# Graph network layers 1 and 2: row exponentials written to DRAM once and loaded spread over all partitions, in place of a spread by TensorE before every quarter

## The chip, the cores and the metric

The kernel runs on one core of one Trainium2 chip. The metric is the device time of one execution in microseconds (us), the median of several runs. TensorE is called PE below, VectorE DVE, ScalarE ACT, GpSimd POOL and SyncE SP. SP does no arithmetic in this kernel; it only issues DMAs.

## The reference

Four graph layers stand one after the other on a node matrix `x` of 4096 x 128 with a 4096 x 4096 adjacency matrix `adj`. Each is fed with `relu(layernorm(x))` and adds its result to `x`.

```python
def _L1_gnn_ref(x, adj, ff0_w, ff1_w, attn_w, g1, b1, g2, b2):   # _ln: normalise, times g, plus b
    x_norm = _ln(x, g1, b1)
    mask = (adj > 0) | jnp.eye(n, dtype=bool)
    for i in range(K):                                             # K = 2 heads
        h = x_norm @ ff0_w[i].T
        s_src = h @ attn_w[i, :c]
        s_dst = h @ attn_w[i, c:]
        e = jax.nn.leaky_relu(s_src[:, None] + s_dst[None, :])
        e = jnp.where(mask, e, jnp.float32(NEG))
        atten = jax.nn.softmax(e, axis=1)
        att = _ln(atten @ h + x, g2, b2)
        h_next = h_next + jax.nn.elu(att @ ff1_w[i].T) / K
    return h_next
...
    Wh = inputs @ W                                                # layer 2 (_L2_gnn_ref)
    e = jax.nn.leaky_relu((Wh @ a[:D])[:, None] + (Wh @ a[D:])[None, :], LRELU_ALPHA)
    att = jax.nn.softmax(jnp.where(adj > 0, e, NEG), axis=-1)
    return jax.nn.relu(att @ Wh)
...
h = jnp.maximum(_layernorm(x, axis=-1), 0.0)
x = x + _L0_gnn_ref(L0_gnn_t, h, adj, ...)       # (degree-normalised adj) @ h, times W, relu
h = jnp.maximum(_layernorm(x, axis=-1), 0.0)
x = x + _L1_gnn_ref(h, adj, ...)
h = jnp.maximum(_layernorm(x, axis=-1), 0.0)
x = x + _L2_gnn_ref(h, adj, ...)
h = jnp.maximum(_layernorm(x, axis=-1), 0.0)
x = x + _L3_gnn_ref(h, adj)                      # adj.T @ h, divided by the column sums
```

## The kernel before

The program names its work by five stages, `run(0, ...)` to `run(4, ...)`: stage 0 is layer 0, stages 1 and 2 are the two heads of layer 1, stage 3 is layer 2 and stage 4 is layer 3. Below, "stage" is always this number. A stage has four quarters `q` of 1024 target nodes each, and a quarter has 32 steps `k`, one for each block of 128 source nodes. All data is float32, apart from the adjacency pattern, which stays in SBUF as the uint8 tile `mask`.

In stages 1 to 3, one step is this. DVE makes a 128 x 1024 tile of unnormalised attention weights, `E = max(R, rank[:, k]) * mask` (L1124), in one of three buffers (`EB = 3`), all part of the tile `ring`. PE multiplies it with the features in `G` and sums in PSUM `acc`: in stages 1 and 2 with the features stationary (L382, two products of 512 columns, each recorded as two instructions), in stages 0, 3 and 4 with the tile stationary (L366, eight products of 129 columns, each recorded as two). `rank` holds an exponential for each source node. `R`, also in `ring`, holds the exponential for each of the quarter's 1024 target nodes, the same row on all 128 partitions: it is what this change is about.

How `R` comes about before the change: for each quarter, ACT copies the quarter's eight columns of `row[h]` to `rq` (`rows_columns`, L772). PE spreads each column over all partitions with a transpose of the column broadcast to 128 x 128 (`spread_rows`, eight transposes, L393) into the PSUM tile `turn`. ACT copies `turn` to `R` in two pieces (`rows_out`, L775 and L776), but not before DVE has made the last tile of the quarter that runs, since that still reads the old `R` (`rows_copy`). There are 14 such spreads: one for each of the 12 quarters of stages 1 to 3 and two more, since the first quarter of stages 1 and 3 has an early row (for its steps 0 to 23, when the last quarter of features is not known) and a late one (steps 24 to 31).

The order on PE is written out by hand. `run(h, q, hooks)` issues the 32 steps, and behind step `k` the hook of that number; the lists `ks` say behind which steps the work of the neighbouring parts stands: `feed` (features of the next stage: `turned` L397 or L409, `project` L420), `post1` (the end of the quarter before: `sums_back` L435, `turned` L397, `apply` L448), and the spreads. DVE has hooks of the same kind. Quarters with a register as index run in a hardware loop (`quarters`). Each engine works in its own order and waits for the others through semaphores: `e_made` (tiles that DVE has made), `e_used` (tiles that PE has read), `rows_spread`, `rows_kept` and so on.

In stages 1 and 3 the first quarter also brings the maximum over all source nodes: DVE's `top_of` (`first`, a maximum over each partition, `second`, the maximum over all, at L1048 after PE's `spread_top`, one transpose).

Of the kernel before, what the change touches and what calls it, by code (L numbers as in the profile page):

```python
# [30 lines left out]
P = 128  # L31
# [33 lines left out]
def graph_layers(nc, x, adj, adj_t, diag, alpha, w0_t, bias0, ff0, ff0_t, ff1_t, attn, g1, b1, g2, b2,  # L65
# [20 lines left out]
    with ExitStack() as ctx:  # L86
# [13 lines left out]
        ident = sb("ident", [P, P])  # L100
        ff1T = sb("ff1T", [P, HEADS, D])
# [19 lines left out]
        w0T = spare[:, 0:D]  # L121
        bias0_b = spare[:, D:2 * D]
# [8 lines left out]
        mean2 = spare[:, o + D + 2:o + 2 * D + 2]  # L131
        fold, later = [spare[:, o + 3 * D + i * S:o + 3 * D + (i + 1) * S] for i in range(2)]
# [34 lines left out]
        kept_rows = {1: 2, 2: 6, 3: 11}  # L167
# [30 lines left out]

        rq_ready, rows_spread, rows_kept = sem("rq_ready"), sem("rows_spread"), sem("rows_kept")
# [70 lines left out]
        def _(sp):  # L270
# [44 lines left out]

            sp.wait_ge(saved, 16 * Q)

            def bring_back(q):
                if fixed(q):
# [37 lines left out]
        def _(pe):  # L357
# [195 lines left out]
            def stage1(q):  # L553
                m = q + kept_rows[1]
# [13 lines left out]
            def stage2(q):  # L568
                m = q + kept_rows[2]
                if fixed(q) and q == 0:  # L570
                    ks = [1, 15, 17, 29]  
                    run(2, q, at(ks, post1(0, Q - 1, m, 2 * Q) + (lambda: spread_rows(m),)))
                    return
# [13 lines left out]
            def spread_mean():  # L587
# [5 lines left out]
            ks = [0, 8, 9, 18, 19, 20, 21, 26, 27]    # L593
            run(3, 0, at(ks, steps + (lambda: spread_top(late_top[3]), lambda: spread_rows(kept_rows[3] - 1), spread_mean,
                                      lambda: spread_rows(kept_rows[3]))))

            def stage3(q):
                run(3, q, {28: lambda: spread_rows(q + kept_rows[3])})
# [831 lines left out]
```

## Time and profile before

| | us |
|---|---|
| median of 3 runs | 1242.03 |
| lowest and highest | 1241.24, 1245.62 |
| the profiled execution | 1240.94 |
| its span | 1239.1 |
| PE busy | 1223.0 (99% of the span) |
| DVE busy | 752.7 (61%) |
| ACT busy | 317.8 (26%) |

Times within the profile count from the start of the span. Stage 1 takes about 262 to 502 us, stage 2 to 759, stage 3 to 1005 and stage 4 to the end. The record of one PE instruction is longer than its share of the engine, since PE begins the next before the last has ended; the distance from one start to the next tells its cost. The chain of work is a view that follows the end of the kernel back to its start, and it gives such distances.

### The profile page before, as it was taken

What the parts mean: (1) busy time and instruction counts of PE and PEld (TensorE: products, weight loads), DVE (VectorE), ACT (ScalarE), POOL (GpSimd) and SP (SyncE); (2) the same over time, 40 slices, a digit from 0 to 9 for tenths busy, and PEclk for the clock granted to TensorE, in tenths of its full rate; (3) what the DMA queues carried; (4) which work ended last, traced back from release to release, by engine and by line L of the source; (5) the groups of instructions that cost most, each with busy time, mean ns of one, the idle gap of its engine ahead of it and who ended that gap; (6) DMA issues with size and microseconds to landing.
All of it is one profiled execution on the core that took longest, in us unless ns stands there. A gap on an engine that the chain in (4) does not pass through costs nothing.

```text
span 1239.1 us, 20060 instructions
## 1 busy us (share of the span) xinstructions
PE 1223.0 (99%) x7953; PEld 967.4 (78%) x7953; DVE 752.7 (61%) x1359; ACT 317.8 (26%) x769; POOL 9.6 (1%) x21
## 2 busy tenths in 40 slices
PE   8999999999999999999999999899999999999998
PEld 8999999964444444444454547899999999999998
DVE  5446554588877777778878787778787840000001
ACT  3312121234433324231424144442312130000000
POOL 3000000000000000000000000000000000000000
PEclk9999999999999999999999999999999999999999
DMA  9888886820000000000000000000000069999810
GB/s 315 275 268 285 281 278 215 275 73 1 17 1 17 0 18 0 17 17 1 1 17 0 17 0 18 1 1 1 1 0 1 1 242 409 410 410 398 294 62 18
DMA packets 47241, 144.33 MB, mean 116 GB/s; under 512 B 4784, under 2 KB 13248, under 8 KB 47168
## 3 DMA queue, kind: packets, MB, share of 16 engines
q1 hardware_dynamic: 42976, 139.08, 31.3%
q10 hardware_dynamic: 3696, 3.67, 0.8%
q8 instruction: 52, 0.85, 0.3%
q0 software_dynamic: 496, 0.55, 0.2%
q14 instruction: 21, 0.17, 0.0%
HBM read 139.09 MB, written 4.19 MB: 116 GB/s over the span
## 4 chain that ended last, share of the span: by engine, by line
PE 87%; DVE 7%; DMA 2%; issue 1%; ACT 1%; SPq 1%; DVEq 0%; ACTq 0%
PE acc L366 51%; PE acc L382 30%; DVE ring L1124 4%; PE mix L420 2%; PE mix L448 1%; PE mix L435 1%; PE turn L397 1%; PE turn L393 1%; ACT V L623 1%; DMA mask<-in_adj_t 1%; SPq L272 1%; DMA mask<-in_adj 1%; DVE stats L960 1%; DVE stats L956 0%; DVE X L1273 0%
## 5 line engine op out<-in xcount | busy, mean ns | idle before, releaser
L1124 DVE SCALAR_TENSOR_TENSOR ring<-ring,score,mask 128x1024 f32<-128x1024 f32 x384 | 482.9, 1281 | 113.1 <-PE acc L382 69.5
L382 PE MATMUL acc<-ring,G 128*128 128x512 f32 x1024 | 450.5, 594 | 3.2 <-DVE ring L1124 2.7
L366 PE MATMUL acc<-G,mask 128*128 128x129 f32 x3584 | 403.5, 275 | 1.6 <-DMA mask<-in_adj 1.1
L366 PEld LDWEIGHTS acc<-G,mask 128*128 128x128 f32 x3584 | 401.5, 192 | 2.1 <-DMA mask<-in_adj 1.5
L382 PEld LDWEIGHTS acc<-ring,G 128*128 128x128 f32 x1024 | 189.3, 190 | 234.0 <-issue 201.5
L366 PE MATMUL acc<-G,ring 128*128 128x129 f32 x2560 | 289.8, 275 | 0.3 <-DVE ring L1124 0.3
L366 PEld LDWEIGHTS acc<-G,ring 128*128 128x128 f32 x2560 | 287.8, 192 | 1.5 <-DVE ring L1124 1.2
L1158 DVE TENSOR_SCALAR mask<-mask 128x1024 uint8<-128x1024 f32 x96 | 64.5, 689 | 53.7 <-DMA mask<-in_adj_t 53.5
L1375 DVE TENSOR_SCALAR zero<-U 128x8 f32<-128x8 f32 x3 | 0.5, 171 | 155.0 <-ACT U L816 155.0
L816 ACT COPY U<-acc 128x387 f32<-128x387 f32 (+1 forms) x36 | 15.6, 446 | 270.9 <-PE acc L366 269.9
L635 ACT ACTIVATE dev<-var 128x8 f32<-128x8 f32 x28 | 5.9, 210 | 266.6 <-DVE var L969 266.6
L1158 DVE TENSOR_SCALAR mask<-ring 128x1024 uint8<-128x1024 f32 x32 | 22.0, 692 | 32.1 <-DMA ring<-in_adj_t 22.2
L623 ACT ACTIVATE V<-X,shift,scale 128x128 f32<-128x128 f32 (+1 forms) x92 | 36.7, 481 | 0.0
L775 ACT COPY ring<-turn 128x512 f32<-128x512 f32 x14 | 8.2, 585 | 109.2 <-DVE ring L1124 64.3
L619 ACT ACT_TABLE_LOAD x26 | 33.4, 1283 | 1.2 <-PEq L1409 0.8
L615 ACT COPY cols<-ident 128x1 f32<-128x1 f32 x40 | 7.6, 190 | 95.8 <-DVE shift L979 35.6
L1394 DVE SCALAR_TENSOR_TENSOR zero<-U 128x3 f32<-128x3 f32 (+1 forms) x3 | 0.5, 161 | 50.8 <-ACT U L816 50.8
L623 ACT ACTIVATE V<-U,shift,scale 128x128 f32<-128x128 f32 x64 | 25.5, 481 | 10.3 <-DVE shift L979 10.3
L420 PEld LDWEIGHTS mix<-ring,U 128*128 128x128 f32 x176 | 20.8, 192 | 2.0 <-issue 1.2
L397 PEld LDWEIGHTS turn<-ident,V 128*128 128x128 f32 x120 | 13.7, 141 | 10.0 <-ACT V L623 5.8
L420 PE MATMUL mix<-ring,U 128*128 128x4 f32 (+2 forms) x176 | 21.0, 265 | 0.0
L397 PE MATMUL turn<-ident,V 128*128 128x128 f32 x120 | 15.7, 274 | 4.1 <-ACT V L623 4.1
(168 smaller groups left out, 548.2 us busy)
## 6 DMA issues: line engine op xcount, KB each, us to landing
mask<-in_adj SPq DMA_DIRECT2D x128, 512.0 KB, 14.9
mask<-in_adj_t SPq DMA_DIRECT2D x96, 512.0 KB, 4.7
ring<-in_adj_t SPq DMA_DIRECT2D x32, 512.0 KB, 4.7
inputs<-V ACTq DMA_DIRECT2D x4, 512.0 KB, 2.7
V<-inputs SPq DMA_DIRECT2D x4, 512.0 KB, 3.9
X<-in_x SPq DMA_DIRECT2D x3, 512.0 KB, 10.6
out_x<-V ACTq DMA_DIRECT2D x3, 512.0 KB, 15.1
X<-in_x SPq DMA_DIRECT2D x2, 256.0 KB, 3.2
```

The lines of the kernel that those rows point to most:

```text
L272: sp.dma_start(X[:, t:t + n, :], x[t * P:(t + n) * P, :].rearrange("(s p) d -> p s d", p=P)).then_inc(loaded, 16)
L366: mm = pe.matmul(acc[:, b, (s % 3) * DW:(s % 3) * DW + DW], lhs[:, s * P:(s + 1) * P], g, start=(k == 0 and s % 3 == 0), stop=(k == T - 1) ...
L382: mm = pe.matmul(acc[:, c, :], g, moving[:, c * BANK:(c + 1) * BANK], start=(k == 0), stop=(k == T - 1), skip_group_check=True)
L393: return pe.transpose(dst, col.broadcast_to([P, P]), ident[:, :])
L397: mm = pe.transpose(turn[:, s * P:(s + 1) * P], V[:, s, :], ident[:, :])
L420: mm = pe.matmul(dst, U[:, s * P:(s + 1) * P], weights, start=True, stop=True, skip_group_check=True)
L435: mm = pe.matmul(mix[:, s // 3, (s % 3) * DW:(s % 3) * DW + DW], U[:, s * P:(s + 1) * P], back_w[h], start=True, stop=True, skip_group_che ...
L619: act.activation(warm[func], ident[:, 0:1], func)
L623: ins = act.activation(dst(s), src(s), func, bias=add(s), scale=mul(s))
L816: act.copy(U[:, b * 3 * DW:b * 3 * DW + w], acc[:, b, 0:w]).then_inc(acc_taken, 1)
L1124: dve.scalar_tensor_tensor(E[k % EB], R, rank[h][:, k:k + 1], span(mask, (q * T + k) * QC, QC), ALU.max, ALU.mult).then_inc(e_made, 1)
L1158: dve.tensor_scalar(span(mask, (q * T + k) * QC, QC), tile0(q, k), 0.0, None, ALU.is_gt).then_inc(mask_made, 1)
```

## The change

Ten of the 14 spreads are gone, those of whole quarters. In their place, three times (once for each of stages 1, 2 and 3), PE turns `row[h]`, 128 x 32, to 32 x 128 in one transpose (`turn_rows`) into `mix`. ACT (stages 1 and 3) or DVE (stage 2) copies that to `turned_rows`; SP writes it to DRAM as 4096 numbers in a row (`write_rows`, 16 KB) and loads from there, for each quarter, the 1024 numbers to all 128 partitions (`load_rows`, 512 KB). They land in `R` or in 1024 columns of `G` that hold nothing at the time (`rows_home`), so that most loads stand a quarter ahead of their use. The early and the late rows of the first quarters of stages 1 and 3 are still spread by PE; the late ones go to a part of `G` (`late_home`), which leaves `R` free for the second quarter's load.

What goes with it: the exponentials `v` of stage 2 move from a column of `G` to `v_second`; a few hooks move by a step or two; DVE's quarters and SP's `bring_back` are no longer in loops; the memset of the last column of `G` for stage 4 is cut in two.

```diff
-        kept_rows = {1: 2, 2: 6, 3: 11}
+        kept_rows = {1: 2, 3: 4}
+        in_third, in_fourth, of_first = [G[:, i, t:t + S, :].rearrange("p s d -> p (s d)")[:, 0:QC]
+                                         for i, t in ((0, 2 * S), (0, 3 * S), (1, 3 * S))]
+        rows_home = {(1, 0): R, (1, 1): R, (1, 2): in_third, (1, 3): in_fourth, (2, 0): R, (2, 1): of_first, (2, 2): R,
+                     (2, 3): of_first, (3, 0): R, (3, 1): R, (3, 2): in_fourth, (3, 3): R}
+        late_home = in_fourth
...
+            def write_rows(h):
+                sp.wait_ge(rows_ready, h)
+                sp.dma_start(given_rows[h - 1].rearrange("(t p) -> t p", p=P), turned_rows).then_inc(rows_written, 16)
+                sp.wait_ge(rows_written, 16 * h)
+
+            def load_rows(h, q):
+                sp.dma_start(rows_home[h, q], given_rows[h - 1, q * QC:(q + 1) * QC].partition_broadcast(P))\
+                    .then_inc(rows_loaded[h, q], 16)
+
+            sp.wait_ge(own_made, Q)
+            write_rows(1)
+            sp.wait_ge(e_made, EARLY)
+            load_rows(1, 1)
+            load_rows(1, 2)
+            sp.wait_ge(e_made, T)
+            load_rows(1, 3)
+            write_rows(2)
+            sp.wait_ge(e_made, 2 * T)
+            load_rows(2, 0)
...
+            sp.wait_ge(*all_summed(1, Q - 1))
+            load_rows(2, 1)
             bring_back(0)
-            quarters(sp, 1, Q - 1, bring_back)
+            sp.wait_ge(e_made, (Q + 1) * T)
+            load_rows(2, 2)
+            bring_back(1)
+            sp.wait_ge(e_made, (Q + 2) * T)
+            load_rows(2, 3)
+            bring_back(2)
+            bring_back(3)
+
+            write_rows(3)
+            sp.wait_ge(e_made, 2 * Q * T + EARLY)
+            load_rows(3, 1)
+            sp.wait_ge(e_made, (2 * Q + 1) * T)
+            load_rows(3, 2)
+            sp.wait_ge(e_made, (2 * Q + 2) * T)
+            load_rows(3, 3)
...
+            def turn_rows(h):
+                pe.wait_ge(r_made, h)
+                pe.transpose(mix[0:T, 2, 0:P], row[h], ident[:, :]).then_inc(rows_turned, 1)
...
-                    ks = [17, 18, 19, 21, 22, 25, 26]  
+                    ks = [17, 18, 19, 21, 22, 24, 26]
                     run(1, q, at(ks, own + (lambda: spread_top(late_top[1]), lambda: spread_rows(1), spread_fold,
-                                            lambda: spread_top(late_top[2]), lambda: spread_rows(m))))
+                                            lambda: turn_rows(1), lambda: (pe.wait_ge(rows_ready, 1), spread_top(late_top[2])))))
                 else:
-                    ks = [2, 15, 17, 29]  
-                    run(1, q, at(ks, post1(0, q - 1, m, 2 * Q) + (lambda: spread_rows(m),)))
+                    ks = [2, 15, 17]
+                    run(1, q, at(ks, post1(0, q - 1, m, 2 * Q)) | more)
             stage1(0)
-            stage1(1)
+            stage1(1, {24: lambda: turn_rows(2)})
+            pe.wait_ge(rows_ready, 2)
...
-                    ks = [1, 13, 15, 26, 29, 27]  
-                    run(2, q, at(ks, steps + (lambda: spread_rows(m, q + 2 * Q),)))
+                    ks = [1, 13, 15, 26, 28]
+                    run(2, q, at(ks, steps))
...
-            ks = [0, 8, 9, 18, 19, 20, 21, 26, 27]  
+            ks = [0, 8, 9, 18, 19, 20, 21, 26, 24]
             run(3, 0, at(ks, steps + (lambda: spread_top(late_top[3]), lambda: spread_rows(kept_rows[3] - 1), spread_mean,
-                                      lambda: spread_rows(kept_rows[3]))))
+                                      lambda: turn_rows(3))))
...
+            def keep_turned(h):
+                act.wait_ge(rows_turned, h)
+                act.copy(turned_rows, mix[0:T, 2, 0:P]).then_inc(rows_ready, 1)
...
             late_rows(1)
-            next_columns(1, 1)
-            feed(2, 2 * Q, 0, [lambda: put_right(1), lambda: exponentials(2), lambda: rows_copy(1, 1)])
+            keep_turned(1)
+            feed(2, 2 * Q, 0, [lambda: put_right(1), lambda: exponentials(2)])
...
-                dve.wait_ge(rows_kept, q + kept_rows[h] - (1 if early else 0))
+                if early:
+                    dve.wait_ge(rows_kept, kept_rows[h] - 1)
+                else:
+                    dve.wait_ge(rows_loaded[h, q], 16)
...
-            quarters(dve, 1, Q - 2, stage3, st, STAGE3)
-            stage3(Q - 1)
+            for q in range(1, Q):
+                stage3(q)
+            dve.wait_ge(e_made, 3 * Q * T)
+            st.mark(dve.memset(G[:, 0, EARLY:T, D], 1.0))
```

Three places in the order of instructions follow. The changed file has other line numbers: its L432 is L382 of before, L443 is L393, L470 is L420, L447 is L397. The first is PE in the first quarter of stage 1, from the spread for the late sums (`fold`) to the end of the quarter; two rows of `acc<-ring,G` are one step, `cols` is `spread_top`, `rq` the row for the second quarter. Before:

```order
L393 MATMUL mix<-ident,ring 128x128 x8
L382 MATMUL acc<-ring,G 128x512 x6
L393 MATMUL mix<-ident,cols 128x128
L382 MATMUL acc<-ring,G 128x512 x2
L393 MATMUL turn<-ident,rq 128x128 x8
L382 MATMUL acc<-ring,G 128x512 x16
```

The same place in the changed kernel:

```order
L443 MATMUL mix<-ident,ring 128x128 x8
L432 MATMUL acc<-ring,G 128x512 x4
L605 MATMUL mix<-ident,score 32x128
L432 MATMUL acc<-ring,G 128x512 x4
L443 MATMUL mix<-ident,cols 128x128
L432 MATMUL acc<-ring,G 128x512 x16
```

The eight transposes of `rq` are gone, one transpose of the whole `row[1]` stands behind step 24, and the transpose of `cols`, for which DVE waits, stands behind step 26 and not 25.

The second place is ACT at the same point of the program, from the copy of the late row. Before:

```order
L775 COPY ring<-turn 128x512
L776 COPY ring<-turn 128x512
L746 COPY U<-mix 128x512
L747 COPY U<-mix 128x512
L772 COPY rq<-score 128x8
L615 COPY cols<-ident 128x1
L623 ACTIVATE V<-X,norms 128x128 x8
L671 DMA inputs<-V 128x1024
L760 ACTIVATE score<-score,cols 128x24
L764 ACTIVATE G<-G,cols 128x1032 x3
```

And in the changed kernel:

```order
L829 COPY G<-turn 128x512
L830 COPY G<-turn 128x512
L800 COPY U<-mix 128x512
L801 COPY U<-mix 128x512
L834 COPY ring<-mix 32x128
L670 COPY cols<-ident 128x1
L678 ACTIVATE V<-X,norms 128x128 x8
L726 DMA inputs<-V 128x1024
L814 ACTIVATE score<-score,cols 128x24
L818 ACTIVATE G<-G,cols 128x1032 x3
```

The copy of the turned rows (L834), which waits for PE's step 24 and the transpose behind it, stands where ACT copied eight columns without a wait, and the normalisation, the save to DRAM and the scaling of `G` (`put_right`) are queued behind it.

The third place is PE at the end of a looped quarter of stage 2, from the turn of the next stage's input. Before:

```order
L397 MATMUL turn<-ident,V 128x128 x8
L483 REGISTER_ALU
L382 MATMUL acc<-ring,G 128x512 x2
L266 REGISTER_ALU
L393 MATMUL turn<-ident,rq 128x128 x8
L483 REGISTER_ALU
L382 MATMUL acc<-ring,G 128x512 x2
L483 REGISTER_ALU
L382 MATMUL acc<-ring,G 128x512 x2
L420 MATMUL mix<-ring,U 128x130 x8
```

And in the changed kernel:

```order
L447 MATMUL turn<-ident,V 128x128 x8
L533 REGISTER_ALU
L432 MATMUL acc<-ring,G 128x512 x2
L533 REGISTER_ALU
L432 MATMUL acc<-ring,G 128x512 x2
L465 REGISTER_ALU
L470 MATMUL mix<-ring,U 128x130 x8
L533 REGISTER_ALU
```

The spread is gone, and the projection into `mix` stands one step earlier, two steps behind the turn.

## Rows read from the trace of the kernel before

**Rows 1.** The page: busy time, share of the span, instructions; granted clock in 40 slices.

```profile
PE 1223.0 (99%) x7953; PEld 967.4 (78%) x7953; DVE 752.7 (61%) x1359; ACT 317.8 (26%) x769; POOL 9.6 (1%) x21
PEclk9999999999999999999999999999999999999999
```

**Rows 2.** The page: chain that ended last, shares of the span by engine.

```profile
PE 87%; DVE 7%; DMA 2%; issue 1%; ACT 1%; SPq 1%; DVEq 0%; ACTq 0%
```

**Rows 3.** Group of spreading transposes on PE: busy us, mean ns, idle before.

```profile
L393 PE MATMUL turn<-ident,rq 128*128 128x128 f32 x112 | 14.6, 273 | 0.5 <-ACT rq L772 0.5
```

**Rows 4.** Chain through a quarter of stage 1: start us, us, what.

```profile
440.95 0.87 PE turn L393 x8
441.82 8.72 PE acc L382 x20
...
501.34 0.88 PE turn L393 x8
```

**Rows 5.** Chain in stages 0 and 3.

```profile
123.39 51.92 PE acc L366 x464
...
941.49 0.87 PE turn L393 x8
942.36 57.19 PE acc L366 x512
```

**Rows 6.** Order of time, PE, end of stage 1's first quarter: start us, us.

```profile
309.49 3.69 PE L382 MATMUL acc<-ring,G 128*128 128x512 f32 x8 [0.27 <-DVE acc L1073]
313.02 0.27 PE L393 MATMUL mix<-ident,cols 128*128 128x128 f32 x1
313.13 1.88 PE L382 MATMUL acc<-ring,G 128*128 128x512 f32 x4
```

**Rows 7.** The same for DVE; in brackets the idle time before and its releaser.

```profile
313.57 0.28 DVE L1048 TENSOR_REDUCE cols<-mix 128x1 f32<-128x128 f32 x1
...
314.17 2.47 DVE L1124 SCALAR_TENSOR_TENSOR ring<-ring,score,mask 128x1024 f32<-128x1024 f32 x2
317.64 1.28 DVE L1124 SCALAR_TENSOR_TENSOR ring<-ring,score,mask 128x1024 f32<-128x1024 f32 x1 [1.00 <-PE acc L382]
...
322.89 1.28 DVE L1124 SCALAR_TENSOR_TENSOR ring<-ring,score,mask 128x1024 f32<-128x1024 f32 x1 [0.63 <-PE acc L382]
```

**Rows 8.** The same for ACT.

```profile
308.02 0.59 ACT L747 COPY U<-mix 128x512 f32<-128x512 f32 x1
...
312.61 3.23 ACT L764 ACTIVATE G<-G,cols 128x1032 f32<-128x1032 f32 x3
...
320.73 0.58 ACT L775 COPY ring<-turn 128x512 f32<-128x512 f32 x1 [4.26 <-DVE ring L1124]
```

**Rows 9.** Chain at the end of a quarter of stage 2.

```profile
620.65 0.87 PE turn L393 x8
...
628.24 1.28 ACT L772
...
630.27 3.70 PE acc L382 x8
```

**Rows 10.** Order of time, DVE, the same place.

```profile
628.61 1.28 DVE L1124 SCALAR_TENSOR_TENSOR ring<-ring,score,mask 128x1024 f32<-128x1024 f32 x1 [3.94 <-PE acc L382]
```

**Rows 11.** DMA issues: KB each, median us from issue to landing.

```profile
mask<-in_adj SPq DMA_DIRECT2D x128, 512.0 KB, 14.9
...
inputs<-V ACTq DMA_DIRECT2D x4, 512.0 KB, 2.7
V<-inputs SPq DMA_DIRECT2D x4, 512.0 KB, 3.9
...
out_x<-V SPq DMA_DIRECT2D x1, 128.0 KB, 1.8
```

**Rows 12.** Order of time, DVE, end of stage 3's first quarter.

```profile
827.81 1.13 DVE L1284 SCALAR_TENSOR_TENSOR mask<-ident,dsub,mask 128x128 uint8<-128x128 f32 x4
829.88 1.28 DVE L1124 SCALAR_TENSOR_TENSOR ring<-ring,score,mask 128x1024 f32<-128x1024 f32 x1 [0.95 <-PE acc L366]
```

More of the change, by code:

```diff
@@ L197, in graph_layers @@
         acc_scaled = sem("acc_scaled")
+        rows_turned, rows_ready, rows_written = sem("rows_turned"), sem("rows_ready"), sem("rows_written")
+        rows_loaded = {at: sem(f"rows_loaded{at[0]}{at[1]}") for at in rows_home if at not in ((1, 0), (3, 0))}
         rq_ready, rows_spread, rows_kept = sem("rq_ready"), sem("rows_spread"), sem("rows_kept")
@@ L726, in exponentials @@
                 act.wait_ge(bias_made, late_top[h])
-                act.activation(G[:, h % 2, lo:T, D], rank[h][:, lo:T], ACT.Exp, bias=vbias, scale=s_).then_inc(v_made, 1)
+                act.activation(v_second if h == 2 else G[:, h % 2, lo:T, D], rank[h][:, lo:T], ACT.Exp, bias=vbias, scale=s_).then_inc(v_made, 1)
                 act.activation(rank[h][:, lo:T], rank[h][:, lo:T], ACT.Exp, bias=wbias, scale=1.0 - s_).then_inc(w_made, 1)
@@ L800, in second_rows @@
                           lambda s: blocks(norms[:, 2, :], q, 1, s), lambda s: blocks(norms[:, 3, :], q, 1, s),
-                          ACT.Identity, f_norm)
+                          ACT.Identity, None)
+                act.copy(blocks(G[:, 0, :, :], q)[:, :, D - 1], span(v_second, q * S, S)).then_inc(f_norm, 1)
             def wide_take(n):
@@ L879, in _, with stage1 @@
             late_rows(1)
[L880 to L884 removed]
+            keep_turned(1)
+            feed(2, 2 * Q, 0, [lambda: put_right(1), lambda: exponentials(2)])
+            def stage1(q):
                 post1(0, q - 1)
[L886 to L891 removed]
+                feed(2, q + 2 * Q, q)
+            quarters(act, 1, Q - 1, stage1)
             post1(0, Q - 1)
[L893 removed]
             def stage2(q, between, beside=()):
@@ L898, in stage2 @@
                 feed(3, q - 1 + 3 * Q, q - 1, between)
-            def stage2_rows(q):
-                next_columns(2, q + 1)
-                stage2(q, [lambda: rows_copy(2, q + 1)])
-            quarters(act, 1, Q - 2, stage2_rows)
+            quarters(act, 1, Q - 2, lambda q: stage2(q, []))
             stage2(Q - 1, [lambda: ready(ACT.Exp)])
@@ L924, in stage3 @@
                 feed(4, q - 1 + 4 * Q, q - 1)
-                if rows:
-                    rows_copy(3, q + 1)
             act.wait_ge(mean_kept, 1)
             quarters(act, 1, Q - 2, stage3)
-            stage3(Q - 1, rows=False)
-            stage3(Q, rows=False)
+            stage3(Q - 1)
+            stage3(Q)
             def store(q):
@@ L1123, in run @@
                         dve.wait_ge(*(all_summed(h - 1, Q - 1) if fixed(q) and q == 0 else all_summed(h, q - 1)))
-                    dve.scalar_tensor_tensor(E[k % EB], R, rank[h][:, k:k + 1], span(mask, (q * T + k) * QC, QC),
+                    dve.scalar_tensor_tensor(E[k % EB], late_home if early and k >= EARLY else rows_home[h, q], rank[h][:, k:k + 1], span(mask, (q * T + k) * QC, QC),
                                              ALU.max, ALU.mult).then_inc(e_made, 1)
@@ L1311, in stage1 @@
                 run(1, q, at(ks, post1(0, q - 1)) | more)
-            stage1(1, {1: scale_norms})
-            quarters(dve, 2, Q - 1, stage1, st, STAGE1)
+            stage1(1, {1: scale_norms, 28: keep_turned})
+            stage1(2)
+            stage1(3)
             ks = [4, 8, 10, 11, 13, 20, 22]
@@ L1328, in stage2 @@
                     run(2, q, at(ks, steps))
-            quarters(dve, 1, Q - 2, stage2, st, STAGE2)
-            stage2(Q - 1)
+            for q in range(1, Q):
+                stage2(q)
             scale_g(3, 0)
@@ L1343, in _ @@
             run(3, 0, at(ks, last[:-2] + feed(3, 4 * Q - 1, Q - 1) + late_steps(3) + [mean_of_all, keep_mean]
-                         + [lambda: st.mark(dve.memset(G[:, 0, :, D], 1.0)) or last[-2](), last[-1]]))
+                         + [lambda: st.mark(dve.memset(G[:, 0, 0:EARLY, D], 1.0)) or last[-2](), last[-1]]))
             def post2(q):
@@ L1366, in stage3 @@
                 run(3, q, at([1, 6, 8, 11, 14, 17], post2(q - 1) + feed(4, q - 1 + 4 * Q, q - 1)))
-            quarters(dve, 1, Q - 2, stage3, st, STAGE3)
-            stage3(Q - 1)
+            for q in range(1, Q):
+                stage3(q)
+            dve.wait_ge(e_made, 3 * Q * T)
+            st.mark(dve.memset(G[:, 0, EARLY:T, D], 1.0))
             for step in post2(Q - 1) + feed(4, 5 * Q - 1, Q - 1):
```

61 lines of the change are left out of this document (25 added, 36 removed).

## The prediction, made before the changed kernel ran

> **What bounds the kernel now.** I read the page's busy times first. PE is busy for 1223.0 of 1239.1 us, at full granted clock in all 40 slices; DVE and ACT are far below [rows 1]. The chain of work runs through PE for 87% of the span and through DVE for 7% [rows 2]. So what is taken off PE counts, unless PE then waits for something in its place. Second, the groups of PE instructions: the transposes that spread rows are 112, which is 14 spreads of eight [rows 3]. Third, the chain, read at the places where a spread stands. In a whole quarter of stage 1 it never leaves PE: from one spread's start to the next are 501.34 - 440.95 = 60.39 us, and the pieces join without a gap [rows 4]. The same holds in stage 3, where 57.19 us of products follow a spread directly [rows 5]. Last, the order of time on PE, DVE and ACT at the four places where instructions change their place [rows 6 to 10, 12].
>
> **What a spread costs.** The group gives 273 ns for one transpose [rows 3], which would make 2.18 us for eight. The chain gives 0.87 or 0.88 us for the same eight [rows 4, 5, 9]: they overlap, and one takes 0.109 us of PE. The start of the products behind them (441.82 after 440.95, 942.36 after 941.49) shows that 0.87 is all that PE loses. I take 0.87. The Trainium skill ("TensorE: Matmul & The Clock Gate", part 4) gives about 275 ns for a transpose in a kernel; that is the record's length here, and by it the ten spreads would be 22 us and not 8.7.
>
> **Removed.** Ten spreads, all on PE's path: 10 x 0.87 = 8.7 us. They are those for the second, third and fourth quarter of each stage and the first of stage 2. With them go ten pairs of copies and ten small copies on ACT. ACT is busy 317.8 us only, so these count just where PE waits for ACT. One such place shows: in stage 2's second looped quarter the chain goes through ACT's L772, a table load of 1.28 us, and PE resumes at 630.27 [rows 9]. PE had projected by 626.76 (620.65 + 0.87 + 3.44 for two steps + 1.80), where that end has in it the tail of a record, up to 0.16 us (0.273 - 0.109), and needed 3.44 for the last two steps: 630.0 to 630.2. I count 0.2 us back there, bounds 0 and 1. The table load itself stays (it moves to the copy of the sums), but ACT reaches it earlier, since `rows_copy` with its wait for DVE is gone.
>
> **Added on PE.** Three single transposes, 0.11 us each, 0.3 us in all; bounds 0.3 and 0.8 (each as long as its record of 0.27).
>
> **Added wait on PE, first quarter of stage 1.** The transpose for `top` stands behind step 26 where it stood behind 25, and also waits for ACT's copy of the turned rows. Before, steps 24 and 25 began at 309.49, the transpose at 313.02 and DVE read it at 313.57, just when it was ready [rows 6, 7]. A step is 1.74 us (8.72 / 20 x 4 [rows 4]). Now step 24 ends at 311.2, the turn at 311.3, step 26 at 314.8, the transpose at 315.0. ACT, free at 308.6 [rows 8], copies at 311.4 and is done by 311.7, so that wait costs nothing. DVE needs 0.6 us from L1048 to its next tile (313.57 to 314.17) and 1.28 for the tile [rows 7]: 315.1 + 0.6 + 1.28 = 317.0. PE ends step 27 at 316.7 and would want the tile of step 28 then. I take a stall of 0.4 us, bounds 0 and 1.7 (a whole step). DVE is not behind later: it idled 1.00 and 0.63 us after this point [rows 7].
>
> **Behind ACT's new wait** are the normalisation, the save, `put_right` and the exponentials of stage 2, all later by 311.7 - 308.6 = 3.1 us. `put_right` ended at 315.8 (312.61 + 3.23) and will end at about 319; DVE and PE want it for the second quarter, from 322.4 on. The exponentials behind it end 3.1 us later too, at about 320; DVE wants them behind its second tile of that quarter. Nothing on PE's path moves; the cover is about 3 us.
>
> **The loads.** The chain for the first one is: turned rows ready (311.7), write of 16 KB, load of 512 KB, then DVE's first tile of the second quarter, at 322.89 before [rows 7] and about 322.4 now. No row shows a load that spreads one DRAM row over partitions or a 16 KB write. Nearest for the write are 1.8 us (128 KB to DRAM) and 2.7 us (512 KB); nearest for the load 3.9 us (512 KB back from DRAM to `V` on the same queue, with the same 4 KB pieces) [rows 11]. 1.8 + 3.9 = 5.7: landed at 317.4, 5.0 us before it is wanted. In stage 3 the tile of the second quarter was made at 829.88 when PE had ended step 30, DVE being free from 828.94 [rows 12]. Step 24 ended six steps (6 x 1.79 by 57.19 / 512 x 16) and a spread earlier, at about 818.1; ready 818.5, landed 824.2, wanted 828.9, 4.7 us over. The other eight loads stand most of a quarter ahead, about 50 us. SP's own order holds no load up: what it waits for ahead of each is past by then. Cost 0; the bound above is the rival below. Ten more loads move 5.2 MB. While stage 0 streamed the matrix, PE took 51.92 / 464 = 0.1119 us for an instruction, against 57.19 / 512 = 0.1117 in stage 3 with hardly any traffic [rows 5], so the traffic itself costs PE nothing.
>
> **DVE's unrolled quarters, the second memset, SP's unrolled `bring_back`.** All off PE's path: DVE waits 3.94 us for PE at the end of a quarter of stage 2 [rows 10]. Cost 0. After the last spread of stage 3's first quarter is gone, PE wants tiles 0.87 us earlier, where DVE has 0.95 us [rows 12]: just enough, bound 0.3.
>
> **Sum.** 8.7 + 0.2 - 0.3 - 0.4 = 8.2 us. The profiled execution, 1240.94 us, becomes 1232.7; the median of the runs stands 1.1 above it, so I forecast 1233.8. Its own range, from the bounds, is 1232 to 1236.
>
> **The rivals.**
> - *Half is given back.* PE reaches each of DVE's crowded stretches with 0.87 us less in hand. If the four spreads of stage 2 and of stage 3's first quarter return as waits for DVE, 4 x 0.87 = 3.5 us are lost: 1237.3. For it: DVE carries 7% of the chain, all in such stretches. Against: DVE idled 3.94 us right before one [rows 10], so the stretches begin from PE's own time. 16%.
> - *Nothing moves.* The spreads were hidden, PE waits the same time elsewhere: 1241 to 1242. Against it are the chain's pieces in stages 1 and 3, without any gap [rows 4, 5]. 10%.
> - *The loads come late.* DVE stands at the start of the second quarters of stages 1 and 3, PE behind it. The matrix loads of stage 4, queued behind each other, take 14.9 us [rows 11]; a load that slow lands at 311.7 + 1.8 + 14.9 = 328.4, 6.0 us late in stage 1 and 6.3 in stage 3: 12.3 - 8.2 = 4.1 slower, 1246. It decides once write and load take more than 10.7 + 4.1 = 14.8 us together. Against it is the 3.9 of [rows 11], with nothing else on the queue. 7%, of which 4% are over 1248. The Trainium skill ("DMA: Bandwidth & Descriptors", latency of one transfer) lays most of a fixed 2 us on the receipt of the write and says that it can be surprisingly long toward HBM; no row here shows the case.
> - *A transpose is worth its record.* If 0.273 us each comes off PE, ten spreads give 80 x 0.273 = 21.8 us: 1220.7. The joins of the chain speak against it [rows 4, 5]. The skill's 275 ns, named above, would have it so. 3%.
> - The forecast keeps 64%.
>
> **Range and chances.** 0.5% of the median is 6.2 us, about what a measurement of this kernel can tell from no change. Faster by more means below 1235.8: the forecast (but 1%), 4 of the 16% and the last rival, 70%. Within it: nothing moves, the rest of the 16%, 3% of the late loads and 1% of the forecast, 26%. Slower: 4%. The range 1231.8 to 1239 holds the forecast and nearly all of the first rival, 79%.
>
> **What would show it.** In the profile of the changed kernel: 32 transposes onto `turn` from `rq` and three of 32 x 128; PE busy near 1215; from quarter to quarter of stage 1 59.5 us in place of 60.4; a gap of about 0.4 us on PE near 317; write and load landing in 5 to 6 us; no idle time of DVE with a DMA as releaser. I am wrong if DVE waits for a load, if PE's idle time grows by over 2 us, or if the chain goes through ACT in stage 1's first quarter.

## The result, and the profile of the changed kernel

| | before | changed |
|---|---|---|
| median of 4 runs beside each other | 1241.63 us (1240.58 to 1245.62) | 1231.01 us (1230.82 to 1234.23) |
| profiled execution, and its span | 1240.94, 1239.1 | 1231.13, 1229.2 |

The ratio is 0.991, with a 95% interval of 0.9894 to 0.9926. The change takes 10.6 us off the median (9.9 off the span) where 8.2 were forecast: 1231.0, which is 0.8 us below the low end of the range. The direction, the mechanism and the main term were right; the sum was too small.

First the page of the changed kernel: busy times, the chain's shares, the groups of transposes, and the new loads (KB each, median us from issue to landing).

```profile
PE 1214.1 (99%) x7876; PEld 959.4 (78%) x7876; DVE 751.9 (61%) x1360; ACT 306.8 (25%) x745; POOL 9.6 (1%) x21
PE 87%; DVE 8%; DMA 2%; ACT 1%; SPq 1%; issue 1%; DVEq 0%
L443 PE MATMUL turn<-ident,rq 128*128 128x128 f32 x32 | 4.2, 274 | 0.5 <-ACT rq L826 0.5
L605 PE MATMUL mix<-ident,score 128*32 128x128 f32 x3 | 0.8, 273 | 0.0
ring<-given_rows SPq DMA_DIRECT2D x5, 512.0 KB, 3.5
G<-given_rows SPq DMA_DIRECT2D x5, 512.0 KB, 3.7
```

80 transposes are gone from the 112 of [rows 3], three single ones have come, and PE is busy for 1214.1 us where I expected about 1215. PE's idle time went from 16.1 to 15.1 us. The PE time removed is 8.9 us, so the span won 1.0 us more than was taken off.

Next, where it went. The chain of the changed kernel, at the first instructions behind a quarter of stage 1 or 2 (start us, us, what):

```profile
390.01 1.78 PE mix L485 x16
...
449.50 1.78 PE mix L485 x16
...
566.84 1.78 PE mix L485 x16
...
629.45 1.78 PE mix L485 x16
...
692.18 1.79 PE mix L485 x16
```

And the same instructions in the chain of the kernel before:

```profile
569.67 1.78 PE mix L435 x16
...
633.97 1.79 PE mix L435 x16
...
698.00 1.78 PE mix L435 x16
```

A quarter of stage 1 takes 449.50 - 390.01 = 59.49 us in place of 60.4, as expected (59.5). But the first looped quarters of stage 2 gained far more than a spread each: 64.30 became 629.45 - 566.84 = 62.61, a gain of 1.69, and 64.03 became 62.73, a gain of 1.30. One spread is 0.87. Taken over the whole span, each stretch from its first tile product's start to that of the next stretch, the gains are:

| stretch | gain, us |
|---|---|
| stage 1's first quarter (a spread, less the turn and the stall) | 0.26 |
| seven quarters of stages 1 and 2 | 6.47 |
| stage 3 (three spreads) | 2.70 |
| stage 4 | 1.40 |
| stage 0 (it ended later) | -0.91 |
| sum | 9.92 |

That is the difference of the spans. Stage 4, whose tile loads and products the change leaves as they were, gave 1.40. PE's order of time there, before (in brackets the idle time and its releaser):

```profile
1004.87 2.05 PE L366 MATMUL acc<-G,mask 128*128 128x129 f32 x16
1008.07 2.16 PE L366 MATMUL acc<-G,mask 128*128 128x129 f32 x17 [1.15 <-DMA mask<-in_adj]
```

and after:

```profile
993.75 2.73 PE L416 MATMUL acc<-G,ring 128*128 128x129 f32 x23
996.35 6.86 PE L416 MATMUL acc<-G,mask 128*128 128x129 f32 x59
```

PE used to stand for the second tile of stage 4's matrix; now it doesn't. The reason stands on SP, in the issues of the first two tiles. Before, and then after:

```profile
1000.89 1.84 SPq L297 DMA_DIRECT2D mask<-in_adj  x2
```

```profile
992.47 0.81 SPq L309 DMA_DIRECT2D mask<-in_adj  x2
```

The first issue of the pair took 0.33 to 0.34 us both times, the second 1.45 before and 0.43 after. Before, one 16-KB packet of instructions ran on queue 8 from 1001.41 to 1002.36, inside the long issue (1001.28 to 1002.73). This is the row of the queue from 1001 to 1003 (packets, MB, share of 16 engines):

```profile
q8 instruction: 1, 0.02, 3.0%
```

That the packet is PE's next instructions, and that it is what holds the issue up, is tested below.

Then the one wait that I had forecast. PE around the moved transpose for `top`:

```profile
315.73 0.27 PE L443 MATMUL mix<-ident,cols 128*128 128x128 f32 x1
315.84 1.88 PE L432 MATMUL acc<-ring,G 128*128 128x512 f32 x4
317.98 1.55 PE L432 MATMUL acc<-ring,G 128*128 128x512 f32 x3 [0.26 <-DVE ring L1166]
```

The transpose stands 0.7 us later than the 315.0 that I worked out, and so does what follows; by the pitch of the steps PE loses 0.42 us at 317.98 (the bracket's 0.26 has the tail of a record in it). Forecast was 0.4. Last, the first row of exponentials on SP's queue: write, then load, and DVE's first tile that needs it.

```profile
312.82 0.34 SPq L330 DMA_DIRECT2D given_rows<-ring  x1
314.25 0.34 SPq L334 DMA_DIRECT2D ring<-given_rows  x1
```

```profile
323.54 1.28 DVE L1166 SCALAR_TENSOR_TENSOR ring<-ring,score,mask 128x1024 f32<-128x1024 f32 x1 [0.41 <-PE acc L432]
```

The write took 1.4 us and the load landed at 318.67, 4.4 us behind its issue: 4.9 us ahead of 323.54, where DVE waits for PE and not for a DMA. All ten loads took 3.3 to 5.5 us.

### The profile page after: what moved, and what is told of

The parts are those of the page before. It is cut to its first block, busy times and chain, and to the rows that moved or that the text cites. A ratio compares the mean times of both kernels' runs of the same rounds, so it can differ in the third digit from the quotient of the medians.

```text
span 1229.2 us, 19400 instructions
## 1 busy us (share of the span) xinstructions
PE 1214.1 (99%) x7876; PEld 959.4 (78%) x7876; DVE 751.9 (61%) x1360; ACT 306.8 (25%) x745; POOL 9.6 (1%) x21
## 4 chain that ended last, share of the span: by engine, by line
PE 87%; DVE 8%; DMA 2%; ACT 1%; SPq 1%; issue 1%; DVEq 0%
PE acc L416 51%; PE acc L432 30%; DVE ring L1166 5%; PE mix L470 1%; DMA ring<-in_adj_t 1%; PE mix L498 1%; PE mix L485 1%; PE turn L447 1%; DMA mask<-in_adj_t 1%; ACT V L678 1%; DVE stats L999 1%; SPq L284 0%; DVE stats L995 0%; DVE X L1315 0%; DVE V L1303 0%
## 5 line engine op out<-in xcount | busy, mean ns | idle before, releaser
L432 PE MATMUL acc<-ring,G 128*128 128x512 f32 x1024 | 449.4, 594 | 2.6 <-DVE ring L1166 2.2
L432 PEld LDWEIGHTS acc<-ring,G 128*128 128x128 f32 x1024 | 190.0, 190 | 235.9 <-issue 205.0
L1166 DVE SCALAR_TENSOR_TENSOR ring<-ring,score,mask 128x1024 f32<-128x1024 f32 x208 | 261.8, 1280 | 55.3 <-PE acc L432 29.0
L1166 DVE SCALAR_TENSOR_TENSOR ring<-G,score,mask 128x1024 f32<-128x1024 f32 x176 | 221.4, 1281 | 47.0 <-PE acc L432 34.2
L859 ACT COPY U<-acc 128x512 f32<-128x512 f32 x16 | 9.4, 586 | 53.1 <-PE acc L432 53.1
L470 PEld LDWEIGHTS mix<-ring,U 128*128 128x128 f32 x176 | 20.8, 192 | 2.0 <-issue 1.2
L447 PEld LDWEIGHTS turn<-ident,V 128*128 128x128 f32 x120 | 13.7, 141 | 10.0 <-ACT V L678 5.8
L470 PE MATMUL mix<-ring,U 128*128 128x4 f32 (+2 forms) x176 | 21.0, 265 | 0.0
```

What stands on the lines that cost most here:

```text
L432: mm = pe.matmul(acc[:, c, :], g, moving[:, c * BANK:(c + 1) * BANK], start=(k == 0), stop=(k == T - 1), skip_group_check=True)
L447: mm = pe.transpose(turn[:, s * P:(s + 1) * P], V[:, s, :], ident[:, :])
L470: mm = pe.matmul(dst, U[:, s * P:(s + 1) * P], weights, start=True, stop=True, skip_group_check=True)
L1166: dve.scalar_tensor_tensor(E[k % EB], late_home if early and k >= EARLY else rows_home[h, q], rank[h][:, k:k + 1], span(mask, (q * T + k) ...
```

## The experiments

**The two kernels again.** Both unchanged, to see which of the gains come again; the changed one was run a third time later.

> The kernel before, profiled a second time, to see which waits of its first profile come back. Two places of the first profile have no part in my prediction: PE stood 1.31 us at the start of stage 4 (the second tile of the matrix landed late on one of its sixteen parts while instructions were being fetched, 1008.07), and in stage 0 PE lost nothing where the changed kernel lost 0.9 us to loads. Theory A (the wait at stage 4 belongs to where the program's instruction fetch falls): it comes back, 1.0 to 1.5 us at the same place, time 1240.5 to 1242. Theory B (chance of one execution): PE's wait there is under 0.4 us in this profile, time 1239.5 to 1241.

> The changed kernel again, for a tighter ratio and a second profile. Theory A: no wait of PE at the start of stage 4, ratio 0.9910 to 0.9925. Theory B: a wait of some size there in this profile, ratio 0.992 to 0.994, near the 8.2 us that I had forecast. Stage 0's loss of 0.9 us to loads is chance by both and may be gone.

> The changed kernel a third time, beside e11 on the same chip: median 1231 to 1232, no fall of the clock in the profile if the shift of the wait keeps it away, no wait of PE at the start of stage 4.

Before: 1242.05 us. Its wait at stage 4's start is there again (PE loses 1.43 us at 1009.19), and its waits in stage 2 are 0.81 at 612 and 0.69 at 676, as in the first profile (0.80 and 0.69). Changed: 1231.75 and 1231.87 us beside 1242.80 and 1242.55, ratios 0.991 [0.9896, 0.9924] and 0.9905 [0.9886, 0.9923]; no wait at stage 4's start in either, and 0.38 us in each of the two places of stage 2. So both extra gains come again; how firmly the one in stage 4 belongs to the kernel is the matter of e3, e5 and e10 below.

e1's profile showed one thing more. PE waits 2.9 us for ACT ahead of the turned block of stage 3, and right behind it the granted clock fell to its lower level (1.2 of 2.4 GHz) for 3.4 us. In the first profile of before it hadn't. The first row is before's, the second e1's (window, its length, busy us of PE, PEld, DVE, ACT, POOL, granted clock, DMA share, GB/s):

```profile
800.00:806.00 6.00, 3.65 (x33) 3.65 (x34) 2.32 (x4) 4.74 (x11) 0.00 (x0) 1.00 0.02 4
```

```profile
799.00:806.00 7.00, 4.35 (x24) 4.35 (x25) 1.89 (x3) 5.28 (x13) 0.00 (x0) 0.76 0.01 4
```

I expected e12 not to show it, since the changed kernel has the wait at another time. It did, and that expectation was wrong:

```profile
796.40:799.80 3.40, 3.40 (x17) 3.40 (x18) 0.04 (x1) 1.32 (x5) 0.00 (x0) 0.54 0.00 0
```

Of the eleven profiles of kernels that keep this wait four show the fall (e1, e4, e10, e12). The Trainium skill ("TensorE: Matmul & The Clock Gate", part 1) ties the clock to how busy TensorE has been recently; the rows agree in that each fall begins within 0.5 us of the end of this wait (in e12 0.3 us ahead of it), and they show as well that the same wait can pass without one.

**DVE's part alone.** The kernel before, with only DVE's quarters written out.

```
-            quarters(dve, 1, Q - 2, stage2, st, STAGE2)
-            stage2(Q - 1)
+            for q in range(1, Q):
+                stage2(q)
```

(and the same in stages 1 and 3)

> The kernel before with one part of the change alone: DVE's quarters of stages 1, 2 and 3 written out in place of hardware loops, spreads and all else as before. Theory A (in a loop, DVE's waits on a register's value and its other register work cost about 0.2 us each, and two of stage 2's looped quarters are bound by DVE for 12 us): PE waits 0.4 us instead of 0.8 and 0.7 at the two crowded stretches of stage 2, 1.0 us gained in all, 1240.6. Rival (what I forecast: nothing, since it is off PE's path): 1241.6. If the wait at stage 4 depends on DVE's code, another 1.3 us.

1241.26 us beside 1242.80, ratio 0.9989 [0.9975, 1.0004]: the timing just allows "nothing" (one of its twelve runs took 4553.63 us and is left out of the ratio). The profile is clearer. PE's waits in the crowded stretches of stage 2 fell from 0.80 and 0.69 to 0.38 and 0.38, those of the changed kernel, and the distances from one quarter's `mix` products to the next quarter's shrank from 64.30 to 63.76 and from 64.03 to 63.60, by 0.54 and 0.43, about 1.0 us in all. The cause is seen on DVE. The looped code of before, between the normalisation and the first tiles of the next quarter:

```profile
603.54 1.22 DVE L1273 SCALAR_TENSOR_TENSOR X<-V,X 128x1024 f32 x1
604.99 1.28 DVE L1124 SCALAR_TENSOR_TENSOR ring<-ring,score,mask 128x1024 f32<-128x1024 f32 x1 [0.23 <-DVE X L1273]
...
611.08 0.17 DVE L969 SCALAR_TENSOR_TENSOR var<-parts 128x8 f32<-128x8 f32 x1
611.30 2.48 DVE L1124 SCALAR_TENSOR_TENSOR ring<-ring,score,mask 128x1024 f32<-128x1024 f32 x2
```

The changed kernel at the same place:

```profile
600.61 1.22 DVE L1315 SCALAR_TENSOR_TENSOR X<-V,X 128x1024 f32<-128x1024 f32 x1
601.86 1.28 DVE L1166 SCALAR_TENSOR_TENSOR ring<-G,score,mask 128x1024 f32<-128x1024 f32 x1
...
607.85 0.17 DVE L1008 SCALAR_TENSOR_TENSOR var<-parts 128x8 f32<-128x8 f32 x1
607.93 2.47 DVE L1166 SCALAR_TENSOR_TENSOR ring<-G,score,mask 128x1024 f32<-128x1024 f32 x2
```

Between `X` and the tile 604.99 - 603.54 - 1.22 = 0.23 us pass in the loop and 0.03 written out; between `var` and the tile 0.05 and -0.09 (the two overlap), so each such step is 0.14 to 0.20 us shorter. In e3, where the row still comes from `ring`, the two gaps are 0.03 and -0.09 as well, so it is the writing out and not the row's new place. In this stretch the chain runs through DVE, so PE gets it all. That these gaps are the waits on a register's value, which the loop needs and the written-out code doesn't, is the difference in the code that fits; only the writing out as a whole was tried.

e3 answers a second question. I had written "if the wait at stage 4 depends on DVE's code, another 1.3 us", and most of it came: the first quarter of stage 4 is 1.00 us shorter than before's, with PE's program unchanged. The fetch runs at 1000.30, 3.35 us ahead of stage 4's first product where it was 3.46 ahead; SP's second issue passes in 0.43 us, and the third is the long one:

```profile
1000.53 1.29 SPq L297 DMA_DIRECT2D mask<-in_adj  x1
```

PE then waits for the third tile, and only 0.3 us. A tenth of a microsecond in the order of the two decides what the fetch costs.

**The spreads put back.** The changed kernel, with ten dead spreads of eight transposes (of an identity column, into `turn`, read by nobody) at the places of the old ones. Nothing waits for them.

```
+            def dead():
+                for s in range(S):
+                    spread(ident[:, s:s + 1], turn[:, s * P:(s + 1) * P])
```

> The changed kernel with ten spreads of eight transposes put back on PE, at the steps where they stood before, of a column that nobody needs (identity), into a tile that nobody reads. It computes more and nothing else. Theory A (a spread costs PE its 0.87 us wherever it stands): 1231.0 + 8.7 = 1239.7. Rival (part of the gain is from ACT's waits and copies, or from rows that are there earlier, and PE's time was partly hidden): 1234 to 1237.

1240.72 us beside 1242.80, ratio 0.998 [0.9971, 0.9989], and 8.97 above e2. The group of the dead ones:

```profile
L443 PE MATMUL turn<-ident 128*128 128x128 f32 x80 | 10.4, 273 | 0.0
```

Each record is 273 ns, and each spread makes its quarter 0.87 to 0.89 us longer. In stage 1's first quarter the stall of 0.42 at 318 goes at the same time, so it adds only about 0.4 net. The wait at the start of stage 4 is back too, 1.17 us. The median holds these two and the fall of the clock besides, so the price is read from the quarters. This prices the main term, and rules out that spreads were hidden or worth their records.

**The start of stage 4.** Theory A: PE's fetch of its next 16 KB of instructions collides with SP's first matrix loads, and falls there or not by how long PE's program is. Theory B: the earlier reads of the changed kernel free SP or the tiles. To tell them apart, only the number of warm-up instructions at PE's start is changed, in both kernels.

```
-    WARM = 38
+    WARM = 94      (the changed kernel, e5)
+    WARM = 110     (the kernel before, e10)
```

> The changed kernel with 94 instead of 38 of the transposes that warm PE up before the first data. They do nothing else. With them PE's program is as long ahead of stages 1 to 4 as with the spreads (56 transposes are the eight of each of the seven spreads in the text of the program), but the spreads stay away. Three profiles with the spreads in PE's program had PE waiting 1.2 to 1.4 us at the start of stage 4, with a fetch of 16 KB of instructions just as SP issues the first loads, and two of the changed kernel had neither. Theory A (the wait hangs on where PE's own instruction fetch falls): the fetch and the wait of 1.0 to 1.5 us are back, the rest of the time from stage 0 on is as in the changed kernel. Theory B (it hangs on what the spreads do to the time or the queues): no wait. The start costs between 0 and 6 us by both.

> The kernel before with 110 instead of 38 warming transposes on PE, spreads and all else as before. 72 transposes more are 144 instructions, and 56 fewer (what the change took out of PE's program) are 112 fewer; 144 + 112 = 256, one fetch of 16 KB at 64 bytes each. So PE's fetches fall on the same instructions of stages 3 and 4 as in the changed kernel. Theory A (the wait at the start of stage 4 hangs on that alone): no fetch near SP's first loads and PE waits under 0.3 us there, with all spreads in place. Theory B (spreads bring the wait): 1.2 to 1.4 us as in both profiles of before. The start costs about 4 to 8 us by both.

The changed kernel so lengthened takes 1236.60 us, beside 1242.51: some 4 us of it are the start itself (the first wide product begins at 265.35, not at about 261), and the wait is back, with all spreads gone:

```profile
1000.74 2.05 PE L416 MATMUL acc<-G,mask 128*128 128x129 f32 x16 [0.16 <-DMA mask<-in_adj]
1003.75 0.94 PE L416 MATMUL acc<-G,mask 128*128 128x129 f32 x6 [0.95 <-DMA mask<-in_adj]
```

Its fetch runs at 997.19 and SP's second issue takes 1.98 us:

```profile
996.57 2.35 SPq L309 DMA_DIRECT2D mask<-in_adj  x2
```

The kernel before, shifted, takes 1248.53 us (one run; 7.5 us of longer start), with all its spreads and no wait there, no fetch near and an issue of 0.43:

```profile
1010.08 0.81 SPq L297 DMA_DIRECT2D mask<-in_adj  x2
```

```profile
1013.92 4.25 PE L366 MATMUL acc<-G,mask 128*128 128x129 f32 x36
```

Theory A holds both ways: the wait goes with where the fetch falls, not with the spreads or the reads. Only PE's program was lengthened and the packet moved, so it is PE's. Where it falls is not all: e3 has before's fetch and 0.3 us of wait, and the changed kernel has a long issue too (1.59 us at 1002.61, beside a fetch), for which PE, with tiles in hand by then, doesn't wait.

**The loads' spare time.** In the changed kernel the loads for the second quarters of stages 1 and 3 are issued when DVE has made all 32 tiles of the first quarter and not when it has made 24 and the row is written. (The load for stage 1's third quarter moves with them; it isn't wanted for another quarter.)

```
-            sp.wait_ge(e_made, EARLY)
+            sp.wait_ge(e_made, T)
             load_rows(1, 1)
```

(and `(2 * Q + 1) * T` ahead of `load_rows(3, 1)`)

> The changed kernel with the loads for the second quarters of stages 1 and 3 issued behind DVE's step 31 and not 23, all others as they are. This takes the cover away. A load of 3.6 to 4.4 us landed 4.9 us before it was wanted in the changed kernel. Theory A (the cover is what makes the loads free, and PE has nothing in hand there): DVE waits for the load 1.5 to 2.5 us at either place and PE as long behind it, 3 to 5 us in all, 1234.5 to 1237. Rival (PE's two tiles in hand hide it): 1231.5 to 1232.5.

1236.59 us beside 1242.51, ratio 0.9954 [0.994, 0.9969], 4.8 above e2. DVE:

```profile
324.46 2.48 DVE L1164 SCALAR_TENSOR_TENSOR ring<-ring,score,mask 128x1024 f32<-128x1024 f32 x2 [2.78 <-DMA ring<-given_rows]
...
826.79 2.48 DVE L1164 SCALAR_TENSOR_TENSOR ring<-ring,score,mask 128x1024 f32<-128x1024 f32 x2 [2.84 <-DMA ring<-given_rows]
```

PE loses 2.30 and 2.66 us there. The loads take their usual time; without their head start DVE waits for them, and that wait reaches PE almost whole. So the loads are free by their place alone.

**The two waits that are left.** e7 fills PE's 2.9 us ahead of stage 3's turned block with 24 idle transposes, so that the clock can't fall behind it. e8 keeps stage 1's turned rows in another PSUM bank, so that the transpose for `top` stands behind step 25 again and doesn't wait for ACT. e9 has both.

```
+            def fill():
+                for _ in range(24):
+                    pe.transpose(turn[:, 0:P], ident[:, :], ident[:, :])
```

```
-                    ks = [17, 18, 19, 21, 22, 24, 26]
+                    ks = [17, 18, 19, 21, 22, 24, 25]
...
```

> The changed kernel with 24 transposes of the identity, 2.6 us, on PE ahead of the wait of 2.9 us in the first quarter of stage 3, into a tile that is free there; they fill an idle time and compute nothing new. In two of the profiles so far, one of the kernel before and one with spreads put back, the granted clock fell to half for 3.4 us right behind that wait, which cost 1.7 us; in the four others it did not. Theory A (the fall follows PE's idle time there and explains why equal kernels differ by 1.5 to 2 us from run to run): never half clock here, all runs within 1.5 us, median 1230.5 to 1231.5, lowest as before. Rival: the same spread and median as the changed kernel, 1231.7.

> The changed kernel with stage 1's turned rows in another PSUM bank, so that the transpose for the maximum stands behind step 25 again and need not wait for the copy of the rows. Theory A (the later place cost the wait of 0.42 us of PE that its profile shows at 317.98): that wait is gone, 0.4 us less, 1231.3, ratio to before lower by 0.0003, which the profile shows and the timing can't. Rival: the wait moves to step 24 or 25, no change.

> The changed kernel with both small edits of the last two: the transpose for the maximum behind step 25, and PE kept busy with 24 idle transposes ahead of its wait in stage 3. Both act apart from each other, so: no wait at stage 1's step 28, no fall of the clock, 1230.8, ratio 0.9900 to 0.9910, all runs within 1.5 us. Rival: no measurable difference from the changed kernel, ratio 0.991, and a spread of 2.5 us as there.

| | median | ratio to before |
|---|---|---|
| e7, filled | 1231.24 | 0.9905 [0.9889, 0.992] |
| e8, `top` behind step 25 | 1231.03 | 0.9907 [0.9892, 0.9922] |
| e9, both | 1230.57 | 0.9898 [0.988, 0.9916] |

In e8 the products run on where the changed kernel stalled; the transpose stands at 313.91 and the steps behind it follow for 6.17 us without a gap:

```profile
313.91 0.27 PE L443 MATMUL mix<-ident,cols 128*128 128x128 f32 x1
314.02 6.17 PE L432 MATMUL acc<-ring,G 128*128 128x512 f32 x14
```

In the profiles of e7 and e9 the clock stays at its upper level there; in e7 PE waits 0.31 us where it waited 2.9. The intervals of all three overlap those of the changed kernel, so by the times none is shown to be faster than it; e9 has the lowest median of all the kernels, 0.4 to 1.3 us under the three of the changed one (1231.01, 1231.75, 1231.87); a stall of 0.4 us and a loss of 1.7 us in some executions would make about that much.

How often the clock fell stands with the timed runs, each of which lists its mean granted clock. Of the profiled runs, those with a fall read 0.998 (e1, e4, e12) or 0.999 (e10), all without one 1.000. At 0.998 or below are 34 of the 63 runs of before that stood beside the experiments, 6 of the 16 of the changed kernel (the result, e2, e12), and none of the 22 of the filled kernels (e7, e9 and e11 below). So the filling does keep the clock up. Before's runs at 1.000 took 1241.3 us on the mean and those at 0.997 1244.9; 0.997 is about two such falls, and no profile here has two, so where the second is stays open.

**Before, filled.** The same 24 transposes in the kernel before.

> The kernel before with 24 idle transposes ahead of its wait of 2.9 us in the first quarter of stage 3, into a tile that is free there, as in the kernel e7. The traces account for 9.9 us of the change, the medians show 10.6 to 11.1. In three of five profiles of kernels with the spreads the clock fell to half behind that wait and 1.7 us were lost, in none of five without spreads. Theory A (falls in about half of the executions of the kernel before account for the rest): no fall here, the median 0.7 to 1.2 us below that of before, ratio 0.999 to 0.9995, and the runs closer together. Rival (the rest is in what differs from run to run in stage 0's loads): same median and spread as before.

1239.65 us beside 1242.55, ratio 0.9974 [0.9964, 0.9985]. This is more than one fall of the clock costs (1.7 us), and the profile says why: the 24 added transposes also moved PE's fetch (to 998.67), and the wait at stage 4's start is gone. Two things changed at once: the profile of before, which has no fall of the clock, is 1.7 us longer than this one's, 1.4 of it in stage 4's first quarter, and none of the twelve runs is at 0.998 or below. What is left of the 2.9 us fits the clock, but this run alone doesn't tell the shares apart.

## Why the prediction was right in kind and too small

Point by point, by its own steps:

- **"I take 0.87" and "Ten spreads, all on PE's path: 10 x 0.87 = 8.7 us."** Right. e4 adds 0.87 to 0.89 for each. The record's length would have been two and a half times too much, and so would the 275 ns of the Trainium skill ("TensorE: Matmul & The Clock Gate", part 4).
- **ACT's place in stage 2, 0.2 us.** 0.25 to 0.28: of the 1.69 us gained in that quarter 0.87 is the spread and 0.54 DVE's, and the product at 630.27 starts 0.68 us behind the one before it (0.43 is usual), in e3 too but not in the changed kernel.
- **Three single transposes, 0.3 us.** About 0.12 where one can be read apart: the quarter with a turn gained 0.79, its neighbour without one 0.91.
- **The wait at `top`, 0.4 us.** 0.42, and gone in e8. Everything there came 0.7 us later than the clock times that I gave, but a stall depends on differences.
- **The loads, 5.0 us ahead.** 4.9, and e6 shows what is behind that cover: 5.0 us of PE's waits over two places. The estimate of write and load was 1.8 + 3.9 = 5.7; it was 1.4 + 4.4 = 5.8. The Trainium skill ("DMA: Bandwidth & Descriptors", "Anatomy of one DMA", on transfers that GpSimd issues) says that the wait for the receipt can be surprisingly long when a write goes to HBM; the three 16-KB writes here, issued by SP, took 1.4 to 2.2 us from issue to landing, so they show no such delay. So my rival of late loads was wrong by its price, not by its mechanism: DVE and PE do stand for a late load.
- These terms together, 8.2 forecast, measured 8.46 (the table's first three rows, less DVE's 0.97).
- **The step that failed: "DVE's unrolled quarters, the second memset, SP's unrolled `bring_back`. All off PE's path", cost 0.** DVE's unrolled quarters are worth 0.97 us in the two looped quarters of stage 2 (0.54 and 0.43), which e3 shows with nothing else changed. I read DVE's 3.94 us of idle time at the quarter's end [rows 10] as cover. It lies ahead of the crowded stretch; behind it DVE works without a break, the chain runs through it (the 7% of [rows 2]), and every gap between two of its instructions is PE's.
- **A term that the sum lacked: the start of stage 4.** 1.40 us. The change touches no load and no product there, and I didn't ask what it moves when PE's program has 56 transposes fewer in its text (a loop's counted once, as in e5). The wait for the second tile hung on one fetch of instructions (e5, e10). This is luck of the layout and not a merit of the change: e5 has the change without it, and e3 has 1.0 us of it without the change to PE's program.
- **8.46 + 0.97 + 1.40 = 10.8**, less 0.9 us of a later end of stage 0, is the 9.9 us between the spans. The medians are 10.6 apart, since the profiled execution of before, one without a fall of the clock, stood 0.7 below its median of these runs. Without the one or the other of the two missing terms the median would have been 1232.0 or 1232.4, inside the stated range of 1231.8 to 1239; it took both to leave it. The own range of 1232 to 1236 was built from the bounds of the terms that I had, and none of them covered a term I didn't have.
- **"Half is given back" was wrong in sign.** PE did reach DVE's crowded stretches earlier, and they took 1.69 and 1.30 us less where they were to take as long: e4's dead spreads cost 0.88 and 0.89 us in these quarters too. DVE was written out in both, so whether something would have been given back with DVE still in loops isn't shown.

What stays open: why stage 0 ended 0.9 us later. Apart from e5 and e10 with their longer start, the starts of the first tile product of stage 1 lie at 259.67 to 260.41 in the profiles of before's kind and at 259.83 to 262.03 in those of the changed one's, by small waits for matrix tiles; nothing tried bears on it. Nor is it shown why the clock fell less often in the changed kernel (6 of 16 runs) than in the kernel before (34 of 63); at 1.7 us a fall, that is some 0.3 us between the two.

## What to carry to other kernels

Price removed TensorE work by the pitch in the chain, from one instruction's start to the next, and check it by putting dead work of the same form back: eight transposes whose records sum to 2.2 us cost 0.87. An engine that idles for microseconds ahead of a crowded stretch is still the bound inside it, so there every edit to its code counts, down to a loop's 0.2-us gaps. And a change of a program's length moves its instruction fetches: look at where they fall in both profiles before a gain in an untouched stage is put down to the change.

## What the runs showed of the hardware that I had not expected

- A 16-KB instruction fetch of PE beside SP's issues of DMAs made one issue take 1.45, 1.81, 1.85 and 1.98 us (before, e1, e4, e5) instead of 0.43, and PE lost 1.2 to 1.4 us to the late tile; in e3 it was 1.29 us on the next issue, and PE lost 0.3. In all five the long issue ended 0.37 us behind the end of the fetch's packet, which lasted 0.95 to 1.37 us, so there the issue waits for the packet. Not every issue does: single ones in stage 0 took their usual 0.33 us beside a fetch (101.21 in before). What the two share isn't told by the records.
- On DVE the looped quarters had gaps of 0.14 to 0.20 us more at a step than the same instructions written out.
- A wait of 2.9 us on PE was followed by 3.4 us at the lower clock in 4 of 11 profiles, at a cost of 1.5 to 1.7 us, and by none in the other 7. With 24 idle transposes in the wait none of three profiles had it, and none of 22 timed runs had a mean granted clock at or below 0.998, where 40 of 79 did without them.
- A load that spreads a row of DRAM over 128 partitions (512 KB written) took 3.3 to 5.5 us in the changed kernel's profile; a plain load of as many bytes took 3.9 [rows 11].
